# Frame merging, projection and state-space stage in one block, convolved rows read where they lie, up product first in expert steps

## The reference

```python
h = _L0_tok_ref(x, ...)                                   # attention over 16 frames -> 8
h = h + _L0_attn_ref(_layernorm(h, axis=-1), ...)         # Mamba block, sequences of 32 rows
h = h + _L0_ffn_ref(_layernorm(h, axis=-1), ...)          # 8 experts, the best 2 for each row
h = h + _L1_attn_ref(_layernorm(h, axis=-1), ...)         # linear attention with decay
h = h + _L1_ffn_ref(_layernorm(h, axis=-1), ...)          # 3 experts, the best 1 for each sequence
```

```python
zxbcdt = u @ W_in
z = zxbcdt[..., :D_INNER]
xBC = zxbcdt[..., D_INNER:D_INNER + D_INNER + 2 * D_STATE]
xBC = jax.nn.silu(_causal_dw_conv(xBC, conv_w, conv_b))
h = dA_t[:, :, None, None] * h + (dt_t[:, :, None] * x_t)[..., None] * B_t[:, None, None, :]
y = jnp.einsum('bhpn,bn->bhp', h, C_t)
yg = y * jax.nn.silu(z)
yn = yg * jax.lax.rsqrt(jnp.mean(jnp.square(yg), -1, keepdims=True) + EPS) * norm_w
return yn @ W_out
```

## Time and profile before

| | us |
|---|---|
| three runs: lowest, median, highest | 552.71, 552.89, 554.67 |
| the profiled execution's own time | 552.83 |
| its span, first to last instruction | 550.7 |
| PE busy, of the span | 503.6 (91%) |
| DVE busy | 367.9 (67%) |
| ACT busy | 258.1 (47%) |
| POOL busy | 225.6 (41%) |

### The profile page before, as it was taken

The page is one execution under the profiler, slowest core; times in us unless marked ns, Lnnn a source line. Parts: engine busy times, 40 slices in busy tenths (PEclk is TensorE's granted clock), DMA queues, the critical chain, the costliest instruction groups (busy, mean ns, idle before and its releaser), DMA issues.

```text
span 550.7 us, 15738 instructions
## 1 busy us (share of the span) xinstructions
PE 503.6 (91%) x5797; PEld 460.2 (84%) x5797; DVE 367.9 (67%) x1045; ACT 258.1 (47%) x737; POOL 225.6 (41%) x327
## 2 busy tenths in 40 slices
PE   8999999988989845999999999999989997999993
PEld 7677777876778734999999999999878887999993
DVE  2676589966989978565666566564447765677671
ACT  2677868763544413333333333332357651645541
POOL 1244420002987833455455555543212224355522
PEclk9999999997999955999999999999999997999998
DMA  9992000008753100113131231220643323122210
GB/s 261 248 199 50 2 1 2 0 0 260 234 175 104 45 30 23 37 53 89 52 89 53 62 80 44 54 45 23 193 153 101 94 88 87 39 72 73 69 39 21
DMA packets 42877, 46.00 MB, mean 84 GB/s; under 512 B 7377, under 2 KB 38226, under 8 KB 42802
## 3 DMA queue, kind: packets, MB, share of 16 engines
q1 hardware_dynamic: 36082, 30.63, 20.6%
q0 software_dynamic: 5760, 12.98, 8.2%
q10 hardware_dynamic: 960, 1.38, 0.9%
HBM read 29.41 MB, written 10.32 MB: 72 GB/s over the span
## 4 chain that ended last, share of the span: by engine, by line
PE 55%; DVE 3%; issue 2%; ACT 2%; DMA 1%; POOLq 0%; POOL 0%; DVEq 0%; ACTq 0%
PE psum L1532 22%; PE psum L1544 20%; PE psum L1923 3%; PE psum L146 3%; PE psum L1514 2%; PE psum L1927 2%; PE psum L1934 1%; ACT rows_turned L1882 1%; PE psum L1680 1%; DVE hidden_room L1282 1%; PE psum L1915 1%; DMA rows_in<-y,token 1%; DVE token_in_tile_pairs L1287 0%; PE psum L1684 0%; PE psum L1689 0%
## 5 line engine op out<-in xcount | busy, mean ns | idle before, releaser
L1532 PE MATMUL psum<-rows_turned,expert_weights 64*128 64x128 f32 x2052 | 128.9, 277 | 0.0
L1544 PE MATMUL psum<-expert_second_weights,hidden_room 64*128 64x192 f32 x1368 | 121.0, 323 | 2.2 <-issue 2.2
L1532 PEld LDWEIGHTS psum<-rows_turned,expert_weights 64*128 64x128 f32 x2052 | 121.4, 191 | 0.3 <-issue 0.2
L1544 PEld LDWEIGHTS psum<-expert_second_weights,hidden_room 64*128 64x128 f32 x1368 | 110.1, 187 | 2.8 <-issue 2.8
L1496 POOL DMA_INDIRECT y<-rows_out,out_row_by_slot x39 | 45.2, 1160 | 73.7 <-DVE rows_out L1626 73.7
L1571 ACT ACTIVATE hidden_room<-psum 128x384 f32<-128x384 f32 x78 | 34.0, 488 | 64.0 <-PE psum L1532 64.0
L1624 DVE COPY rows_out<-psum 128x192 f32<-128x192 f32 x39 | 13.9, 358 | 57.8 <-PE psum L1544 57.8
L1489 POOL DMA_INDIRECT rows_in<-x,token x39 | 43.4, 1113 | 21.9 <-issue 11.6
L1557 ACT ACTIVATE rows_turned<-psum 128x192 f32<-128x192 f32 x57 | 18.9, 332 | 64.1 <-PE psum L1514 64.1
L786 PE MATMUL psum<-arena 97*128 97x512 f32 (+1 forms) x192 | 47.0, 400 | 1.1 <-ACT sz L813 0.5
L1569 ACT ACTIVATE hidden_room<-psum,expert_weights 128x128 f32<-128x128 f32 x108 | 29.9, 376 | 31.4 <-PE psum L1532 31.3
(11 more groups left out here) (278 smaller groups left out, 982.1 us busy)
## 6 DMA issues: line engine op xcount, KB each, us to landing
xbc_tile<-xbc SPq DMA_DIRECT2D x16, 320.0 KB, 3.4
w_proj<-in_w_proj SPq DMA_DIRECT2D x8, 576.0 KB, 5.5
sz<-in_x SPq DMA_DIRECT2D x16, 192.0 KB, 7.3
w_fc<-in_w_fc SPq DMA_DIRECT2D x4, 768.0 KB, 18.8
w<-in_w SPq DMA_DIRECT2D x3, 576.0 KB, 4.0
w_fc<-in_w_fc SPq DMA_DIRECT2D x4, 384.0 KB, 17.3
x<-xf_tile SPq DMA_DIRECT2D x16, 96.0 KB, 1.6
expert_rows<-y SPq DMA_DIRECT2D x8, 192.0 KB, 3.8
```

The lines of the kernel that those rows point to most:

```text
L1532: done = nc.tensor.matmul(ps_h[t.odd][half][:, ch, :], w_now[at, t.odd, first:first + P], xt[at, t.odd, block, :], start=block == 0 and ch ...
L1544: done = nc.tensor.matmul(ps_y[half], hid[at, t.odd, ch, :], w_down_now[at, t.odd, ch * D:(ch + 1) * D], start=ch == 0, stop=ch == HC - 1)
```

## The change

- The state-space stage no longer has a block of its own: `state_space` gives back five functions (a `Stage`), which `merge_frames` calls behind its own work on each engine. There is one block where there were two. Its small tiles lie where the tiles of `merge_frames` were.
- SP copies no rows; PE reads `s.xbc` in place, behind waits for the silu of the stretch in question (`silu_done`) and, for tile 0, for the taps that read the banks it writes to.
- All 16 tiles are written out; there is no loop and no register index.
- The 28 filler matmuls go; 16 stand behind `decay_and_bc` of tile 0, after the last silu of the gate.
- The scaling of `w_out` moves from DVE to POOL.
- The loads of `w_proj` wait for the first `mixing`; SP does not wait for the stored rows at the end of the stage, POOL waits for them before its first gather.
- In the expert steps PE runs `up` first, then `turn_rows`, then `down`, in both expert stages.

```diff
-                merge_frames(nc, dram, m, s, banks, project_in(nc, m, s, banks, both))
-            state_space(nc, dram, m, s, w, ps)
+                projection = project_in(nc, m, s, banks, both)
+                merge_frames(nc, dram, m, s, banks, projection, state_space(nc, dram, m, s, w, ps, projection, -(-nc.sbuf_base // 32) * 32))
...
                 projection.tensor(pe)
+                mixing.tensor(pe)
...
-        pe.wait_ge(taps_done, 3 * (5 * (STRETCHES - 1) + 1))
-        stay_busy(nc, banks[0][:, 0:P], m.c["ident"], 28)
...
+            if t.i == 0:
+                sp.wait_ge(mix_done, 1)
...
-                pipelined(sp, TILES, [(8, store), (0, copy_tile), (2, load_next)], 12, straight=True)
-                for sent in row_sent:
-                    sp.wait_ge(sent, 16 * TILES // 2)
+        pipelined(sp, TILES, [(2, load_next), (8, store)], 12, straight=True)
...
+            if t.i == 0:
+                pe.wait_ge(projection.taps_done, 3 * 16)
             pe.wait_ge(upto_done, t.i + 1)
             need(pe, exp_done, t.i)
             nc.tensor.matmul(ps_d, c["after"], a_upto[:, t.odd, :, :].rearrange("p h t -> p (h t)"), start=True, stop=True).then_inc(d_mm, 1)
-                    pe.wait_ge(xb_in[t.odd], 16 * (t.k + 1))
+            if t.i == 0:
+                pe.wait_ge(projection.taps_done, 3 * 17)
+            pe.wait_ge(projection.silu_done, min(20, 5 * (t.i // 4 + 1)))
...
-                    nc.tensor.matmul(ps_g, xb[:, t.odd, 3, :], xb[:, t.odd, 4, :], start=True, stop=True)
+            nc.tensor.matmul(ps_g, s.xbc[:, 3, tokens(t.i)], s.xbc[:, 4, tokens(t.i)], start=True, stop=True)
...
+        def wait_busy(t):
+            if t.i == 0:
+                pe.wait_ge(projection.gate_out, 12)
+                stay_busy(nc, ps_none, c["ident"], 16)
...
+        pipelined(pe, TILES, [(6, add_squares), (3, mix_time), (9, turn), (10, route), (5, project_out), (1, decay_and_bc), (1, wait_busy)], 12, straight=True)
...
+    def gpsimd(pool):
+        pool.wait_ge(m.w_out_loaded, 16)
+        for ch in range(3):
+            nc.gpsimd.tensor_scalar(m.w_out[:, ch, :], m.w_out[:, ch, :], p["norm_w"][:, ch:ch + 1], None, ALU.mult).then_inc(wo_ready, 1)
+        pool.wait_ge(projection.dt_a_set, 1)
...
-        pipelined(pe, n_tiles, [(1, turn_rows), (2, up), (3, down)], 4, straight=True)
+        pipelined(pe, n_tiles, [(2, up), (1, turn_rows), (3, down)], 4, straight=True)
```

More of the change, by code:

```diff
@@ L130, in need @@
         eng.wait_ge(sem, value)
-def need_alone(eng, m, *counts):
-    counts = [(sem, value if isinstance(value, int) else eng.snap(value)) for sem, value in counts]
-    if not all(isinstance(value, int) for _, value in counts):
-        eng.wait_ge(m.loaded, 16)
-    for sem, value in counts:
-        need(eng, sem, value)
 def stay_busy(nc, to, of, count):
@@ L178, in build @@
             run_first = experts(nc, m, ps, 1, E1, T1, late, shared, m.expert1, m.token1, m.out_row1, first, dram["x1"], dram["y1"], m.w_fc, w.w_proj, None,
-                                ACT.Gelu_apprx_tanh, ((m.w_fc_loaded, 16 * STACK_LOADS), (w.w_proj_loaded, 16 * E1)), load_next=lambda sp, t: w.load_next(sp, t, dram))
+                                ACT.Gelu_apprx_tanh, ((m.w_fc_loaded, 16 * STACK_LOADS), (w.w_proj_loaded, 16 * E1)), load_next=lambda sp, t: w.load_next(sp, t, dram),
+                                rows_there=[(sent, 16 * TILES // 2) for sent in m.x1_sent])
             folded = fold_weights(nc, m, ps, late)
@@ L183, in build @@
             run_second = experts(nc, m, ps, 2, E2, T2, late, shared, m.expert2, m.token2, m.out_row, second, two_rows(dram), dram["out"], w.w1, w.w2, w.b2,
-                                 ACT.Gelu, ((w.w1_loaded, 16 * (STACK_LOADS + 1) * E2), (w.w2_loaded, 16 * (E2 + 1))), merge=m.score_slot, rows_there=attention)
+                                 ACT.Gelu, ((w.w1_loaded, 16 * (STACK_LOADS + 1) * E2), (w.w2_loaded, 16 * (E2 + 1))), merge=m.score_slot, rows_there=attention.rows_sent)
             with nc.Block() as block:
@@ L267, in __init__ @@
         self.wg_loaded = ctx.enter_context(nc.semaphore("wg_loaded"))
+        self.x1_sent = [ctx.enter_context(nc.semaphore(n)) for n in ("x1_sent_even", "x1_sent_odd")]
 class Placed:
@@ L349, in semaphore, with merge_frames @@
         return self.semaphores[-1]
-def merge_frames(nc, dram, m, s, banks, projection):
+def merge_frames(nc, dram, m, s, banks, projection, mixing):
     with ExitStack() as ctx:
@@ L433, in _ @@
                 sp.dma_start(m.w_qkv[0:HD, :, 3 * D + 1 + E2:], dram["wg"].rearrange("(c p) e -> p c e", p=HD)).then_inc(m.wg_loaded, 16)
+                mixing.sync(sp)
             @block.tensor
@@ L613, in _ @@
                 projection.scalar(act)
+                mixing.scalar(act)
             @block.vector
@@ L708, in _ @@
                 projection.vector(dve)
+                mixing.vector(dve)
             @block.gpsimd
@@ L732, in _ @@
                 pipelined(pool, TILES, [(4, roots)], 8, straight=True)
+                mixing.gpsimd(pool)
+@dataclass
+class Stage:
+    tensor: Callable
+    scalar: Callable
+    gpsimd: Callable
+    vector: Callable
+    sync: Callable = lambda sp: None
+    tokens_set: object = None
+    experts_set: object = None
+    rows_set: object = None
+    rows_out: object = None
+    rows_sent: object = ()
+    logits_set: object = None
 @dataclass
@@ L742 @@
     exp_a: Callable
+    taps_done: object
+    gate_out: object
+    silu_done: object
+    dt_a_set: object
     tensor: Callable
@@ L1500, in gpsimd @@
         if rows_there:
-            for sent, value in rows_there.rows_sent:
+            for sent, value in rows_there:
                 pool.wait_ge(sent, value)
```

422 lines of the change are left out of this document (198 added, 224 removed).

## The result

The changed kernel took 562.61 us (median of 4 runs, 561.40 to 567.36), the kernel before 552.90 on the same occasion (4 runs, 552.71 to 554.67): a ratio of 1.0184, 95% interval 1.0121 to 1.0248. So it was slower by about 1.8% where 542.0 was forecast. Timed again on three other occasions, the same kernel took 540.72, 558.68 and 539.05. Ratios leave out single executions far above the rest: some of the kernel before at a lower granted clock (up to 584.44 us), and one of the 12 of the third timing, 1696.88 us, which nothing here explains. So there are two things to explain: why the kernel was slower than forecast, and why only on two of four occasions.

What follows compares the result with a forecast made beforehand. It took the state-space stage's head as the loss, DVE's pace as binding its middle, and PE without gaps in expert stages. Gains 6.4 + 1.9 + 1.3 + 0.2 + 1.0 = 10.8 off 552.83 gave 542.0 us, range 538.7 to 545.6.

Steps and rivals of the forecast that it cites:

- The seam: Between projection and state-space stage: block boundary and 28 fillers go, first `mixing` at 120.83 instead of 127.19; gain 6.4 us.
- Tiles 1 and 2: Head of the state-space stage: the two steps after tile 0's `mixing` shorten from 5.83 us; gain 1.9, bounds minus 1.8 and 1.9.
- the likeliest case: Main forecast, 542.0 us, chance 0.63: at the state-space head, 16 fillers leave PE no idle time and its clock holds.
- The copies: State-space stage: 16 row-copy DMAs go, so DVE's and PE's waits shrink; gain 1.3 us, bounds 0 and 1.8.
- POOL's scaling: `w_out` scaling beside DVE's taps, before the state-space stage: taken as 0; minus 0.8 us by the bare row.
- Start of the first expert stage: New order starts the first up a microsecond earlier, but little reaches the second up; gain 0.2 us, bounds 0 and 1.0.
- Second stage: Start of the second expert stage: the first up begins earlier; gain 1.0 us, bounds 0 and 3.2.
- the clock holds: Second expert stage: one PE pause goes, so the first up takes 2.1 us, not 4.1; 540.0 us, chance 0.12.
- The step that failed: Steady expert steps, 4.19 us a tile: claimed no group waits, so the new order gains nothing there.
- ACT's new order cannot do it: Expert steps: claimed ACT's copies-then-gelu order cannot cause the slowdown, since 4.37 us lie between a tile's up and down.
- the rival on the slower side: Expert steps: turn between up and down breaks both PE overlaps, 0.34 us a tile, 19.4 in all; 561.4, chance 0.03.

Runs made afterwards that it cites:

- the change with POOL's two waits: Changed kernel with gathers issued only behind the down product's signal and scatters only behind the turn's; 541.20, then 538.89 and 539.43 us, no late updates.

## Why the prediction was wrong, and where it was right

Against the fourth timing, where nothing was late, the terms can be read off.

- *The seam*, forecast 6.4: 6.55 (127.19 to 120.64; 6.33 in the first timing). *Tiles 1 and 2*, forecast 1.9: 2.02 (5.83 to 3.81). Right, and the clock and the fillers behaved as the likeliest case had it: the granted clock was 1.00 from 120 to 130 us, although three of five of PE's instructions per tile there are transposes.
- *The copies*, forecast 1.3 with bounds 0 and 1.8: tiles 3 and 4 gave 0.27 (5.73 to 5.46), where the prediction had them at DVE's pace as before, and the way from the `mixing` of tile 4 to that of tile 15 is 1.69 shorter (138.75 to 182.87 before, 129.91 to 172.34 now). Together 1.96: undersized by 0.7, and over the bound. Another 0.3 lies between there and the first turn, which makes 10.8 in all (219.48 to 208.66).
- *POOL's scaling*, forecast 0: it ran at 73.8 to 76.2 us in the first timing, beside taps of the first stretch, and three taps beside it took 2.21 together, where one takes 0.72. Right.
- *Start of the first expert stage*, forecast 0.2: 164.82 to 164.76, 0.06. *Second stage*, forecast 1.0 with 3.2 as the bound if the first up keeps the full clock: 79.91 to 76.89, 3.0. Of this 1.1 came without the new order (78.83 in the change with the turn first). The rival "the clock holds" came true in the change; with the order alone it did once (first up 2.28, stage 76.89) and once did not (3.69 and 78.48). In the first timing the first up kept the clock too and the second lost it, as shown above. Timeline of PE in the second timing of the change, against 4.10 in the earlier trace rows and 3.91 in the change with the turn first:

```profile
456.23 2.28 PE L1534 MATMUL psum<-rows_turned,expert_weights 64*128 64x128 f32 x36
...
459.42 2.28 PE L1534 MATMUL psum<-rows_turned,expert_weights 64*128 64x128 f32 x36 [0.73 <-ACT rows_turned L1561]
```

- Sum: 10.8 + 0.1 + 3.0 is 13.9, and 552.83 less 13.9 is 538.9. The timings without late updates are 540.72 and 539.05; the forecast was 542.0, with a range from 538.7 to 545.6. So the sum holds where no update is late. The terms that were too small (the copies by 0.7, the second stage by 2.0) account for most of the difference.

**The step that failed** is "in the steady state each of the three groups is as long as its columns and none waits, so the order gives nothing". Each group is as long as its columns, but the sentence costs the order by what waits now, not by what is left before something waits. With the turn ahead of up, the rows turned in one step are asked for a whole step later. With the turn behind up they are asked for in the next 2.2 us, of which ACT needs most; 0.93 is left. On two of four occasions the turn's update came over a microsecond late in most steps, 1.22 and 1.13 on average over the first stage, and most steps became 0.3 to 0.8 longer: 17.0 + 7.3 is 24.3 us, and 563.37 less 24.3 is 539.1.

Two sentences beside it were wrong for the same reason. "ACT's new order cannot do it" looked at gelu and its down product, 4.37 us apart, and not at the take and the next up, where the new order of PE, not of ACT, had cut the distance. And the rival on the slower side gave 561.4, close to the 562.61 measured, by a mechanism that is not there: overlaps on PE are not broken (down follows the turn by 0.18 in every step, late or not). The near number is chance.

What no row of the kernel before could show is the lateness: its updates were on time to 0.01 us on average. What they could show is the slack, by adding up the loop up, turn, take, up for the new order.

## What to carry to other kernels

A new order of steps that are all covered is not free: add up the loop it closes and write down the slack it leaves, against the slack of the old order. Here 0.93 us decided 20 us. Where two timings of one program differ by more than their spread (here 562.61 and 540.72), compare the waits of an engine with the records of what it waits for before explaining the program. The kernel to use is the change with PE's order turn, up, down (540.66 and 542.65, on time and not), or the change with POOL's two waits (541.20, 538.89, 539.43) once it has been seen with late updates; only half of it was.

## What the runs showed of the hardware

- TensorE's semaphore updates can come over a microsecond behind the last product: up to 1.76 (up) and 1.87 (turn) us late in the change, on some occasions only, with the same program and a granted clock no lower (0.971 at its first timing, 0.964 at its second). The Trainium skill, "Perfetto Trace Analysis", section on the tensor engine instruction, says that a matmul's reported end is computed from its size, and that the update is pushed when PSUM has acknowledged the writes; the traces agree that record and update are two things (the record ends 0.38 after the turn's start, the update came 1.71 after it), and do not show what held the update back.
- The late ones are those due beside POOL's issues of indirect DMAs; moved away, 0.15 on average. Gathers alone, with DVE idle, sufficed for 1.18; scatters alone gave up to 0.55. Whether the issue or its transfer does it, and why only some occasions have late updates, is not shown.
- Down's updates, due in most steps when POOL issues nothing, were never late by more than 0.27 in the changed kernel, though they follow the turn's late ones within a microsecond. With the turn first a gather's issue reaches them in the second stage, and they were up to 0.70 late.
- A late update can cost the clock as well: after 2.39 us without work PE's granted clock was 0.57 for the next up product, 3.81 us instead of 2.28.
